# Expert weights of the last feed-forward stage: forty tiles read theirs from SBUF, filled by DMA from a DRAM scratch, instead of from a selector matmul

## The reference, cut to what matters

```python
combine = jnp.zeros((T, E), xf.dtype).at[jnp.arange(T)[:, None], topk_idx].add(tw)

def expert_step(acc, inp):
    gu, dn, c = inp
    g = xf @ gu[:I].T
    u = xf @ gu[I:].T
    o = jax.nn.silu(g) * u @ dn.T
    return (acc + c[:, None] * o, None)
routed, _ = jax.lax.scan(expert_step, jnp.zeros_like(xf), (experts_gate_up, experts_down, combine.T))
sh = jax.nn.silu(xf @ shared_gate_w.T) * (xf @ shared_up_w.T)
shared_out = sh @ shared_down_w.T
return (routed + shared_out).reshape(b, s, h)
```

## Time and profile before

| | before |
|---|---|
| median of 3 runs | 1268.76 us (1267.93 to 1269.71) |
| the profiled execution, its own time | 1269.89 us |
| span of the profiled execution | 1268.1 us |
| mean granted TensorE clock | 0.96 |
| PE busy | 1142.7 us, 90% |
| DVE busy | 741.2 us, 58% |
| ACT busy | 702.3 us, 55% |
| POOL busy | 415.7 us, 33% |
| mean DMA rate | 13 GB/s |

### The profile page before, as it was taken

How to read it: one execution, slowest core, us unless ns; L and a number is a source line. 1 busy time by engine, 2 the same in 40 slices (tenths; PEclk the granted TensorE clock), 3 DMA queues, 4 the chain that set the end, 5 groups by cost and what they waited for, 6 DMA issues and landing times. The chain is left out here.

```text
span 1268.1 us, 24927 instructions
## 1 busy us (share of the span) xinstructions
PE 1142.7 (90%) x9793; PEld 844.3 (67%) x9793; DVE 741.2 (58%) x1589; ACT 702.3 (55%) x1284; POOL 415.7 (33%) x601
## 2 busy tenths in 40 slices
PE   1879799699999999999998789979869997999998
PEld 0668357578888888888885556654536664466667
DVE  5858646455556556566561479974638994622224
ACT  2578541265666656666665256766346775644440
POOL 3200001133332323444444334421543532644441
PEclk9889799899999999999999899999979998999999
DMA  4500000100000000000000000000000000000000
GB/s 171 196 1 1 1 1 1 67 1 1 2 1 2 1 2 1 2 1 2 1 2 1 1 2 2 2 2 1 1 1 2 2 2 1 1 1 9 10 1 17
DMA packets 6529, 16.31 MB, mean 13 GB/s; under 512 B 1312, under 2 KB 3568, under 8 KB 5520
## 3 DMA queue, kind: packets, MB, share of 16 engines
q1 hardware_dynamic: 6416, 14.74, 3.2%
HBM read 13.69 MB, written 1.05 MB: 12 GB/s over the span
## 5 line engine op out<-in xcount | busy, mean ns | idle before, releaser
L1188 POOL TENSOR_TENSOR work<-work 128x1024 f32<-128x1024 f32 x64 | 121.3, 1896 | 275.8 <-DVE work L1281 275.8
L1268 DVE TENSOR_REDUCE work<-psum 128x8 f32<-128x1024 f32 x64 | 78.0, 1219 | 95.5 <-PE psum L1077 95.5
L1211 ACT ACTIVATE work<-work 128x1024 f32<-128x1024 f32 x64 | 67.4, 1053 | 98.3 <-DVE work L1272 98.3
L1279 DVE TENSOR_REDUCE work<-work 128x8 f32<-128x1024 f32 x64 | 77.4, 1209 | 70.3 <-ACT work L1211 70.3
L1615 PEld LDWEIGHTS psum<-w_down,work 128*128 128x128 f32 x768 | 99.5, 191 | 24.5 <-issue 22.0
L957 ACT ACTIVATE work<-psum 128x512 f32<-128x512 f32 x128 | 72.8, 596 | 62.5 <-PE psum L836 61.6
L1615 PE MATMUL psum<-w_down,work 128*128 128x128 f32 x768 | 100.6, 275 | 0.7 <-DVE x L1716 0.7
L995 DVE TENSOR_REDUCE work<-psum 128x8 f32<-128x1024 f32 x64 | 75.4, 1219 | 33.2 <-PE psum L822 33.2
L1708 DVE TENSOR_TENSOR work<-psum,big 128x512 f32<-128x512 f32 x69 | 47.3, 690 | 81.0 <-PE psum L1590 79.2
L836 PEld LDWEIGHTS psum<-ident,work 128*128 128x128 f32 x512 | 56.5, 141 | 43.1 <-issue 27.9
L1272 DVE TENSOR_TENSOR work<-psum,work 128x1024 f32<-128x1024 f32 x64 | 78.4, 1225 | 6.4
(11 more groups left out here) (336 smaller groups left out, 2646.0 us busy)
## 6 DMA issues: line engine op xcount, KB each, us to landing
x<-in_x SPq DMA_DIRECT2D x1, 1024.0 KB, 4.9
ctx_tok<-in_ctx SPq DMA_DIRECT2D x1, 1024.0 KB, 6.9
ctxt<-in_ctxt SPq DMA_DIRECT2D x1, 1024.0 KB, 10.5
mask<-in_mask SPq DMA_DIRECT2D x1, 1024.0 KB, 7.4
w_down<-in_down SPq DMA_DIRECT2D x1, 1024.0 KB, 6.6
ctx_tok<-in_g SPq DMA_DIRECT2D x1, 1024.0 KB, 5.5
big<-in_u SPq DMA_DIRECT2D x1, 1024.0 KB, 7.5
out<-x SPq DMA_DIRECT2D x4, 256.0 KB, 2.2
```

What stands on the lines that cost most here:

```text
L1188: pool.tensor_tensor(prob[:, u % 2, h, :], prob[:, u % 2, h, :], rinv[:, u % 2, h].unsqueeze(2).broadcast_to([P, 8, P]), ALU.mult)\
L1211: act.activation(p, p, ACT.Exp).then_inc(S["exp"], 1)
L1268: dve.tensor_reduce(nmax[:, u % 2, h], s, AX.X, ALU.max, negate=True).then_inc(S["max"], 1)
L1279: dve.tensor_reduce(rsum[:, u % 2, h], prob[:, u % 2, h, :], AX.X, ALU.add).then_inc(S["sum"], 1)
```

## The change

For tiles 8 to 50, without the shared ones (16, 33, 50), which are forty (`sent`), `weigh` takes the weights from SBUF instead of PSUM. PE no longer selects for them. The weights come by another way: `turn_back` now also transposes the float32 weights themselves for groups 0, 1 and 2 (`whole`, four 128x32 blocks, 32 output partitions), `keep` copies those into `chosen` (SBUF that held a mask of an earlier stage), SP stores each group's [32, 512] to a DRAM scratch, waits for all three stores, and then loads for each tile two rows of the scratch, each broadcast to 64 partitions, into one of four buffers (`WR = 4`). A buffer is filled again when DVE has weighed the tile that used it (`made`). Tiles 0 to 7 and the 16 weighted tiles of group 3 (51 to 66) are still selected, so `combt` is made for groups 0 and 3 only. The turns are now five: group 0 in parts, groups 0, 1, 2 whole, group 3 in parts. The stores of x to the output stand between the loads on SP. There are five more semaphores.

```diff
--- before.py
+++ after.py
@@ -115,6 +115,7 @@
         self.w = {}
         self.sels = sb("sels", [P, 2048], BF16)
         self.combt = sb("combt", [P, T], BF16)
+        self.chosen = self.mask2[0:32, :].bitcast(F32)
         self.own, self.cleared = [], []
         self.work = sb("work", [P, 13 * 1024])
         self.xn = self.work[:, 0:T]
@@ -1336,7 +1337,10 @@
 
     NONE, MARK = -3e38, 3e38
 
-    def __init__(self, k, a, tag, E, groups, top_groups, top, kind, gate_w, rbias=None, factor=1.0):
+    def __init__(self, k, a, tag, E, groups, top_groups, top, kind, gate_w, rbias=None, factor=1.0, spread=False):
+        self.spread = spread
+        self.turns = [(0, False), (0, True), (1, True), (2, True), (3, False)] if spread else \
+            [(g, False) for g in range(NG)]
         self.k, self.E, self.G, self.top_groups, self.top = k, E, groups, top_groups, top
         self.kind, self.gate_w, self.rbias, self.factor = kind, gate_w, rbias, factor
 
@@ -1356,7 +1360,7 @@
         self.tot, self.best = a.take(NB), take(8)
         self.parts = a.take((3 * NB * E + 1) // 2).bitcast(BF16).rearrange("p (t q e) -> p t q e", t=NB, q=3)
         self.S = {n: k.sem(f"{tag}_" + n) for n in
-                  ("logit", "st", "turn", "chain", "shift", "exp", "parts", "turn2", "comb")}
+                  ("logit", "st", "turn", "chain", "shift", "exp", "parts", "turn2", "comb", "stored")}
 
     def logits(self, pe):
         k, S = self.k, self.S
@@ -1372,12 +1376,16 @@
             mm = pe.transpose(k.bank[5][:, c * P:(c + 1) * P], self.st[:, c * P:(c + 1) * P], k.ident[:, :])
         mm.then_inc(S["turn"], 1)
 
-    def turn_back(self, pe, g):
+    def turn_back(self, pe, n):
         k, S, rows = self.k, self.S, 3 * self.E
+        g, whole = self.turns[n]
         pe.wait_ge(S["parts"], 1)
-        if g:
-            pe.wait_ge(S["comb"], g)
+        if n:
+            pe.wait_ge(S["comb"], n)
         for c in range(GB):
+            if whole:
+                mm = pe.transpose(k.bank[7][0:self.E, c * P:(c + 1) * P], self.w[:, GB * g + c, :], k.ident[:, :])
+                continue
             mm = pe.matmul(k.bank[7][0:rows, c * P:(c + 1) * P],
                            self.parts[:, GB * g + c, :, :].rearrange("p q e -> p (q e)"), k.ident16[:, :],
                            start=True, stop=True)
@@ -1393,9 +1401,14 @@
         act.wait_ge(self.S["shift"], 1)
         act.activation(self.w, self.s, ACT.Exp).then_inc(self.S["exp"], 1)
 
-    def keep(self, act, g):
+    def keep(self, act, n):
         k, S, rows = self.k, self.S, 3 * self.E
-        act.wait_ge(S["turn2"], g + 1)
+        g, whole = self.turns[n]
+        act.wait_ge(S["turn2"], n + 1)
+        if whole:
+            act.activation(k.chosen[0:self.E, g * GT:(g + 1) * GT], k.bank[7][0:self.E, :], ACT.Copy)\
+               .then_inc(S["comb"], 1)
+            return
         act.activation(k.combt[0:rows, g * GT:(g + 1) * GT], k.bank[7][0:rows, :], ACT.Copy)\
            .then_inc(S["comb"], 1)
 
@@ -1514,6 +1527,11 @@
     r = Route(k, a, tag + "r", **routing) if routed else None
     H = J if one_down else 3
     h3 = a.take(H * GT, "p (n c) -> p n c", n=H) if routed else None
+    by_dma, WR = routed and r.spread, 4
+    spread = a.take(WR * GT, "p (n c) -> p n c", n=WR) if by_dma else None
+    landed = [k.sem(f"{tag}_weights{n}") for n in range(WR)] if by_dma else None
+    sent = [n for n in range(8, N - J) if n % J < J - 1] if by_dma else []
+    selected = [n for n in range(N) if tiles[n % J][3] is not None and n not in sent]
     u = a.take(2 * GT, "p (n c) -> p n c", n=2) if second else None
     if not last_sub:
         xn = a.take(2 * GT, "p (n c) -> p n c", n=2)
@@ -1582,11 +1600,11 @@
 
             def select(n):
                 g, j = divmod(n, J)
-                if weighted[j]:
-                    c = made(n) - 1
-                    pe.wait_ge(r.S["comb"], g + 1)
+                if n in selected:
+                    c = selected.index(n)
+                    pe.wait_ge(r.S["comb"], r.turns.index((g, False)) + 1)
                     if c >= 2:
-                        pe.wait_ge(S["made"], c - 1)
+                        pe.wait_ge(S["made"], made(selected[c - 2]))
                     pe.matmul(bank[4 + c % 2][:, :], tiles[j][3], k.combt[:, g * GT:(g + 1) * GT],
                               start=True, stop=True).then_inc(S["sel"], 1)
 
@@ -1640,7 +1658,7 @@
                     up(m + ahead)
                 if m < N:
                     select(m)
-                if routed and 1 <= m < NG:
+                if routed and 1 <= m < len(r.turns):
                     r.turn_back(pe, m)
                 if 0 <= m - LAG < N:
                     down(m - LAG)
@@ -1698,15 +1716,21 @@
 
             def weigh(n):
                 c = made(n) - 1
-                dve.wait_ge(S["sel"], c + 1)
+                if n in sent:
+                    s = sent.index(n)
+                    weights = spread[:, s % WR, :]
+                    dve.wait_ge(landed[s % WR], 32 * (s // WR + 1))
+                else:
+                    s = selected.index(n)
+                    weights = bank[4 + s % 2][:, :]
+                    dve.wait_ge(S["sel"], s + 1)
                 wait_ready(dve, n)
                 if c >= H:
                     if one_down:
                         dve.wait_ge(S["down"], (n - H) // 2 + 1)
                     else:
                         dve.wait_ge(S["down"], weighted_tiles[c - H] + 1)
-                dve.tensor_tensor(h3[:, c % H, :], bank[4 + c % 2][:, :], ring[n % R], ALU.mult)\
-                   .then_inc(S["made"], 1)
+                dve.tensor_tensor(h3[:, c % H, :], weights, ring[n % R], ALU.mult).then_inc(S["made"], 1)
 
             def add(g):
                 xg = k.x[:, g * GT:(g + 1) * GT]
@@ -1805,12 +1829,36 @@
         if last_sub:
             @block.sync
             def _(sp):
-                for g in range(NG):
+                def store(g):
                     sp.wait_ge(S["added"], g + 1)
                     sp.dma_start(k.out[:, g * GT:(g + 1) * GT], k.x[:, g * GT:(g + 1) * GT])\
                       .then_inc(S["stored"], 16)
+
+                def keep_chosen(g):
+                    of = slice(g * GT, (g + 1) * GT)
+                    sp.wait_ge(r.S["comb"], r.turns.index((g, True)) + 1)
+                    sp.dma_start(k.dram["chosen"][:, of], k.chosen[:, of]).then_inc(r.S["stored"], 16)
+
+                def spread_weights(n):
+                    g, j = divmod(n, J)
+                    s = sent.index(n)
+                    if s >= WR:
+                        sp.wait_ge(S["made"], made(sent[s - WR]))
+                    for half in range(2):
+                        sp.dma_start(spread[64 * half:64 * half + 64, s % WR, :],
+                                     k.dram["chosen"][2 * j + half:2 * j + half + 1, g * GT:(g + 1) * GT]
+                                     .broadcast_to([64, GT])).then_inc(landed[s % WR], 16)
+
+                for g in range(NG - 1):
+                    keep_chosen(g)
+                sp.wait_ge(r.S["stored"], 16 * (NG - 1))
+                for n in sent:
+                    if n >= J and n % J == 8:
+                        store(n // J - 1)
+                    spread_weights(n)
+                store(NG - 2)
+                store(NG - 1)
                 sp.wait_ge(S["stored"], 16 * NG)
-
 
 
 class Requantise:
@@ -1947,7 +1995,7 @@
             k.stage(feed_forward, "f3", 7, tiles, ACT.Silu, ahead=16, lags=(0, 0, 0),
                     spare=(k.big[0], k.big[2], k.negb, k.ctxt),
                     routing=dict(E=32, groups=8, top_groups=4, top=6, kind="sigmoid", gate_w=w["gate3"],
-                                 rbias=k.rows[:, R_SB:R_SB + 32], factor=2.5))
+                                 rbias=k.rows[:, R_SB:R_SB + 32], factor=2.5, spread=True))
         else:
             stored = k.sem("stored")
             with nc.Block() as block:
@@ -2030,6 +2078,7 @@
     arrays = {f"in_{n}": v for n, v in layout(inputs).items()}
     dram = {n[3:]: nc.dram_tensor(n, v.shape, mybir.dt.from_np(v.dtype), kind="ExternalInput").ap()
             for n, v in arrays.items()}
+    dram["chosen"] = nc.dram_tensor("chosen", (32, T), F32, kind="Internal").ap()
     out = nc.dram_tensor("out", (P, T), F32, kind="ExternalOutput").ap()
     build(nc, dram, out)
     r = run_bass_kernel_spmd(nc, [arrays], core_ids=[0])
```

## The result

The executions of before and after do not overlap:

| | before | after |
|---|---|---|
| median of 4 runs each | 1269.24 us (1267.93 to 1269.83) | 1262.36 us (1260.33 to 1264.08) |
| ratio after / before | | 0.9947, 95% interval 0.9929 to 0.9964 |
| the profiled execution, its own time | 1269.89 us | 1264.08 us |
| span of the profiled execution | 1268.1 us | 1262.2 us |
| mean granted TensorE clock | 0.96 | 0.964 |

A forecast was written before the change was run, and what follows sets the result against it. PE was taken to bound the stage; -8.6 (selectors) + 0.88 (turns) + 0.36 (clears) = -7.4 us, so a median of 1261.4 us from 1268.76. Likeliest range 1259.9 to 1262.4 us, high end extended to 1265.5.

The forecast's parts named there:

- PE bounds the stage: In this last stage PE sets the pace, 2.82 us a tile; time leaving PE is gained in full.
- The selectors: PE's selector matmuls removed from forty tiles at 0.216 us each, passes becoming 2.61 us: -8.6 us.
- The turns: On PE, two turns of the parts at 0.22 us go, three float32 turns at 0.44 us come: +0.88 us.
- the upper bound: Float32 turn on PE priced at 0.44 us, giving 0.88 in sum; the lower bound, if 32 partitions are cheaper, was 0.22.
- The clears: Five more semaphores for POOL to clear at the end of the span, 0.071 us each, uncovered: +0.36 us.
- DVE and POOL: With both inputs of `weigh` in SBUF they exclude each other, together 1.96 us of 2.61 a tile: cost 0.
- SP and the DMAs: SP's loads for the forty tiles hold nobody: 0.9 us issue a tile, six us of lead, cost 0.
- The threshold of 3.1 us a pair: Slowest loading of a tile's pair that costs nothing; at 3.3 us a pair the whole gain is gone.
- The first rival: SP's queue: each load lands before the next moves, 4.4 us a pair, kernel slower at 1315 us; chance 5%.
- The suspicion of the repeated row: Loads reading one 2 KB row 64 times might be slow: 109 GB/s, 2.40 us a pair, or 4.4 if held up.
- The share of the DMA engines: In the changed profile's last slices, some 100 GB/s at a DMA share of about 0.25.
- the likeliest case: The forecast's own case for the median, 1259.9 to 1262.4 us, given 85%.

The follow-up runs named there:

- run 2: Changed kernel, all DMAs kept, but in the forty tiles DVE multiplies by PSUM banks instead of the loaded weights: 1261.14 us, stage 163.9 us.
- run 1: Changed kernel without the DRAM scratch, its loads and the three whole turns, the forty tiles multiplied by a constant: median 1261.62 us, stage 162.5 us.
- run 11: run 8 with twelve buffers instead of eight and group 2's store moved behind the last load on SP: median 1257.63 us, stage 158.4 us.
- run 5: Changed kernel with every pair of loads issued a second time into buffers nobody reads: 1272.4 us, stage 174.0 us.
- run 7: Changed kernel with the last group's sixteen tiles also loaded by DMA, eight buffers and the last turn whole: median 1260.91 us, stage 163.0 us.
- run 8: run 7 plus loads from tile 3, twelve unused semaphores not allocated, last group's sums in their own PSUM bank: median 1260.18 us, stage 160.6 us.
- run 3: Changed kernel with one buffer for the loaded weights instead of four: 1323.99 us, stage 227.6 us.
- run 10: Changed kernel plus one extra 256 KB transfer a tile from x to 64 partitions of unread buffers: 1263.15 us, stage 164.3 us.
- run 6: Changed kernel whose loads read 64 different rows of x instead of one scratch row 64 times: 1264.6 us, stage 163.9 us.
- run 12: run 5 with the second pair of loads reading 64 different rows of x each instead of one repeated row: 1262.95 us, stage 164.3 us.
- run 4: Changed kernel with two buffers for the loaded weights instead of four: median 1261.98 us, stage 163.7 us.

## Why the prediction was right

The sign, the mechanism and the size of the stage's gain held, -7.5 us measured against -7.4. Step by step:

**PE bounds the stage.** Right, and shown from both sides: relief of DVE (run 2) and of the DMAs (run 1) gave nothing beyond the whole turns, and with more selectors off PE (run 11) the gain grows as their price says.

**The selectors, -8.6 us.** Right: passes of 2.61 us as pass 50 had before.

**The turns, +0.88 us.** Right: 0.44 us each, the upper bound, and run 1 got the three back with 1.4 us for 1.32. Fewer output partitions make a turn no cheaper.

**The clears, +0.36 us.** Right: 2.4 us against 2.0.

**DVE and POOL, 0.** The cost is right, a detail was wrong. I had both at 1.96 us together, with POOL partly stretched. POOL kept its 1.27 us, starting first by 0.3 us, and DVE alone took 1.5 us. The rows that foretold it were those of the 1.71 us in the earlier trace rows; the stretched POOL of the other row needs DVE to be first. The order of the two starts decides who pays. The rule of the Trainium skill, "SBUF — State Buffer", section "SBUF: two separate sides", an exclusive lock that goes to the one that starts first, fits that and the end of `weigh` behind POOL's (1161.95 against 1161.41). That the loser is blocked fully is not quite so here: the 0.54 us are less than the 0.69 that `weigh` takes alone.

**SP and the DMAs, 0.** Right. Tile 8 was weighed at 1121.30 in a pass that began at about 1121.0 (forecast 1119.5, in an execution that was 1.6 us behind). Its loads were issued at 1111.0 and 1111.5 and land in 2.9 us, so with the six us of lead that were forecast. The threshold of 3.1 us a pair was never near: a pair costs 1.6 us even at the limit that run 5 found. I had taken 2.40 us from a window of the start as the nearest row. That window was a bound on what had been asked for there, not on what the queues can do. An issue of 0.45 us was the price behind a pause only: the second of a pair takes 0.60, so a pair costs SP 1.1 us and not 0.9. It cost nothing here and became the limit in runs 7 and 8.

**The first rival, one load after the other.** Refuted by run 3 (4.15 us a round with one buffer, release and `weigh` included) and by run 10, where three quarters of 192 GB/s went to one half of the partitions. The Trainium skill, in "SBUF — State Buffer", section "Can I just issue two DMAs to hit both halves?", has such transfers serialize, with 6% over a single one. The steady 98 to 192 GB/s could not tell, since the page's figure for 64 partitions, which the prediction gives, is 196. The start of run 10 can: from 1113 to 1120 us its transfers, all to 64 partitions, moved 250 GB/s, where an estimate from the page's two figures is 208. So the page's rule does not hold here. The suspicion of the repeated row was right in kind: it costs, but only beyond 162 GB/s, 1.6 times what the kernel asks for.

**The share of the DMA engines** came out at 0.31, not 0.25. The estimate scaled the window of the start (109 GB/s at 0.50) down by guess; it hung on nothing.

**The median** came out at 1262.36 us, 1.0 above the 1261.4. That is not a term of the stage: before was remeasured at 1269.24, 0.5 above its earlier median, and the rest is within the spread of the four executions, 1260.33 to 1264.08. So the forecast of the median was missed by more than that of the stage, and the 1262.36 lie at the very end of the likeliest case (to 1262.4). The terms of the sum cannot be told apart by the medians, only by the stage.

What stays open is why the loads of run 5 stop at 162 GB/s: whether by the repeated row, by the two rows lying next to each other, by the scratch as a tensor of its own, or by what repeats in the descriptors was not tried.

## What to carry to other kernels

When the bounding engine makes an operand that depends on nothing late, let DMAs bring it: one pass of the trace with the piece already missing gives the gain, and the count of buffers times the period, against issue plus landing, says whether it is safe. Keep the lead for the stretch in which the period is shortest, here the last group with 0.89 us a tile against 1.2 us of SP, and move stores that wait for late results behind the loads. Judge such a change on the stage's own stretch; two profiled executions differed by 1.6 us before the change had even begun.

## What the runs showed of the hardware

- Loads that all read the same rows of 2 KB of a DRAM scratch flow at 98 GB/s like any others (share 0.31 against 0.32 for different rows), but at doubled demand they stop at 162 GB/s with a share of 0.81 and landing of 6.7 us; with half of them on other rows, of another tensor, the same issues and bytes reach 192 GB/s at a share of 0.65 and 3.1 us (runs 5, 6, 12).
- The share of the DMA engines is no measure of headroom in bytes: 0.31 at 98 GB/s, 0.65 to 0.78 at 192 to 195, 0.81 at 162.
- SP issues a load of 64 rows in 0.44 us behind a pause and in 0.60 us right behind another issue. In run 5, where the loads back up, the median is 0.69 us. Single long issues say nothing: the longest are 1.76 us in after and in run 12 and 1.68 in run 5.
- A POOL multiplication that starts 0.3 us before DVE's with both inputs in SBUF keeps its 1.27 us, and DVE's goes from 0.69 to 1.50 us.
- The spread between executions lies ahead of this stage: in the profiles of after and of runs 2, 4 and 6 it starts at 1098.3, 1095.5, 1100.4 and 1098.8, and it lasts 163.9, 163.9, 163.7 and 163.9 us. At its ends it goes with the mean granted clock: of eleven executions of the kernel before, the span of the shortest was 1266.0 us at 0.970 and that of the longest 1271.7 at 0.957. In between the order is not strict: of eleven others, one took 1268.2 us at 0.960 and one 1270.1 at 0.964.
